# One transformer decoder layer with routed experts: GpSimd handles group 1's rows and routing ahead of group 0's scatters

## The reference

```
x = layernorm(x + attn_block(x))          # linear attention (16 heads of 8) and a GELU FFN
x = layernorm(x + cross_attn(x, ctx))     # softmax attention, per-head norm, rotary queries
x = layernorm(x + ffn(x))                 # 8 experts, two for each token
```

```
h   = mod(int(x[:, 0] + x[:, 1]), 8)                 # first expert of a token
sel = [h, mod(h + 1, 8)]
out = sum over e in sel of 0.5 * (relu(x @ W1[e] + b1[e]) @ W2[e] + b2[e])
```

## Time and profile before

| | us |
|---|---|
| median of 3 runs | 330.95 |
| lowest, highest | 326.02, 331.38 |
| the profiled execution | 324.2 |
| its span, first to last instruction | 322.4 |

### The profile page before, as it was taken

The page is one execution under the profiler, slowest core; times in us unless marked ns, Lnnn a source line. Parts: engine busy times, 40 slices in busy tenths (PEclk is TensorE's granted clock), DMA queues, the critical chain, the costliest instruction groups (busy, mean ns, idle before and its releaser), DMA issues. The chain is left out here.

```text
span 322.4 us, 7292 instructions
## 1 busy us (share of the span) xinstructions
PE 262.2 (81%) x2341; PEld 193.9 (60%) x2341; DVE 179.2 (56%) x634; ACT 152.8 (47%) x375; POOL 117.6 (36%) x191
## 2 busy tenths in 40 slices
PE   0697867878999978788888989595399999999980
PEld 0376656744354346444454555384389999999970
DVE  4641564942025464697778791359336666566650
ACT  2234215345689781557667766312044444444440
POOL 4000004800432441346312717577324333444441
PEclk9999999969999995999999999879599999999996
DMA  7910103810599675327690001051222200000000
GB/s 217 271 43 15 55 0 100 180 17 1 143 237 234 204 142 139 47 63 137 204 198 3 3 3 37 2 157 41 58 53 75 75 25 16 16 19 11 5 16 16
DMA packets 26641, 26.43 MB, mean 82 GB/s; under 512 B 2895, under 2 KB 23120, under 8 KB 26610
## 3 DMA queue, kind: packets, MB, share of 16 engines
q1 hardware_dynamic: 24996, 23.25, 30.1%
q0 software_dynamic: 1328, 2.75, 2.5%
q10 hardware_dynamic: 288, 0.07, 0.1%
HBM read 16.93 MB, written 9.29 MB: 81 GB/s over the span
## 5 line engine op out<-in xcount | busy, mean ns | idle before, releaser
L1200 DVE TENSOR_REDUCE M<-ps 128x4 f32<-128x512 f32 x64 | 42.7, 685 | 16.7 <-PE ps L650 16.6
L1015 ACT ACTIVATE CTX<-ps 128x512 f32<-128x512 f32 x64 | 37.8, 602 | 25.7 <-PE ps L685 18.8
L1056 ACT ACTIVATE KPK<-ps,EB 128x128 f32<-128x128 f32 x80 | 24.7, 359 | 37.1 <-PE ps L827 29.5
L838 PE MATMUL ps<-EW,KPK 128*128 128x128 f32 x320 | 39.5, 276 | 0.0
L827 PE MATMUL ps<-QPK,EW 128*128 x320 | 39.1, 275 | 0.4 <-ACT QPK L1041 0.4
L1528 POOL DMA_INDIRECT out_dram<-ADD,tok_u x21 | 21.1, 1005 | 48.9 <-DVE ADD L1360 48.9
L827 PEld LDWEIGHTS ps<-QPK,EW 128*128 128x128 f32 x320 | 37.3, 192 | 0.7 <-issue 0.7
L838 PEld LDWEIGHTS ps<-EW,KPK 128*128 128x128 f32 x320 | 37.2, 191 | 0.0
L416 PE MATMUL ps<-C 128*128 128x128 f32 x160 | 25.5, 318 | 8.0 <-DMA sorted_scratch<-KVS,posu 8.0
L685 PE MATMUL ps<-QPK,KPK 49*128 49x128 bf16 x256 | 25.3, 219 | 4.8 <-ACT CTX L1015 2.5
L416 PEld LDWEIGHTS ps<-C 128*128 128x128 f32 x160 | 23.4, 228 | 9.4 <-issue 9.0
(11 more groups left out here) (215 smaller groups left out, 495.3 us busy)
## 6 DMA issues: line engine op xcount, KB each, us to landing
k_packed_scratch<-PART SPq DMA_DIRECT2D x24, 128.0 KB, 2.4
KPK<-k_packed_scratch SPq DMA_DIRECT2D x8, 384.0 KB, 6.4
q_packed_scratch<-PART SPq DMA_DIRECT2D x24, 128.0 KB, 2.5
QPK<-q_packed_scratch SPq DMA_DIRECT2D x8, 384.0 KB, 5.8
EW<-in_eW_dram SPq DMA_DIRECT2D x1, 2048.0 KB, 11.4
KPK<-sorted_scratch SPq DMA_DIRECT2D x24, 66.0 KB, 1.8
X<-in_x_dram SPq DMA_DIRECT2D x4, 256.0 KB, 3.9
C<-in_constants_dram SPq DMA_DIRECT2D x1, 720.0 KB, 6.5
```

Source lines behind the costliest of these rows:

```text
L838: last = mm(ps[:, 4, 0:P], HE[:, c, :], EW2[:, e, c % NF, :], start=(c == 0), stop=(c == 2 * NF - 1))
L1015: A(EXPS[:, u % 4, :], ps[:, 2 + u % 2, :], ACT.Exp).then_inc(s_exp, 1)
L1056: last = A(HE[:, c, :], ps[:, k, (c % 2) * P:(c % 2 + 1) * P], ACT.Relu, bias=EB1[:, h, c:c + 1])
L1200: nc.vector.tensor_reduce(M[:, b % RING, c:c + 4], bank_rows(u % 2), AX.X, ALU.max).then_inc(s_max, 1)
```

## The change

On GpSimd the call of `scatter(0)` moves from behind `route(0)` to behind `route(1)`. Nothing else differs: the operations, tiles and semaphores are the same, and the waits within `scatter(0)` stay with it.

```diff
             normalise_rows(0)
             route(0)
-            scatter(0)
             normalise_rows(1)
             route(1)
+            scatter(0)
             scatter(1)
             normalise_rows(2)
             scatter(2)
```

## The result

The changed kernel takes 328.56 us in the median of 20 runs (323.08 to 335.23), the kernel before 327.47 in the median of as many (320.03 to 331.38). The ratio is 1.010, with a 95% interval of 1.006 to 1.014. So it is slower by 1%, where 0.992 was forecast: it moved the other way. That 328.56 us is nearly the forecast 328.4 is luck: the forecast was counted from the 330.95 us of three runs, and twenty runs put the kernel before at 327.47.

The account below looks back on a forecast made before the run. The chain to the sixteenth scatter was taken as bound, with GpSimd's queue limiting after the change: 5.4 us earlier, 3.2 given back, 0.3 added, 2.55 gained. Span 319.9 (318.9 to 320.5; all cases 316.1 to 324.0), median 328.4 us (322.5 to 331.0).

Parts of the forecast that it names:

- step 2: TensorE's and VectorE's chain to posu of group 2 moves 3.61 to 6.3 us earlier, ready between 213.0 and 215.7.
- Step 1: GpSimd starts group 1 at 192.43; route(1) ends at 202.32, 5.4 us earlier, removing TensorE's 3.61 us wait.
- Steps 3 and 4: GpSimd after route(1): gap 0.8, eight scatters 9.93, normalise_rows(2) 3.15, gap 0.8 us, then scatter(2) at 217.05.
- step 4: At scatter(2), GpSimd becomes the bound, starting it 2.55 us earlier; wrong if VectorE still releases it.
- Step 5: The last scatter lands at 228.4 instead of 230.97; register loads and slot loop move earlier as a block.
- rival (b): Slot loop or scatter landing gives part back through TensorE's half clock; net gain 0.6 to 1.3 us; chance 0.17.
- (a): All of the TensorE and VectorE chain's gain reaches the end, 3.6 to 6.3 us; chance 0.08.
- (d): At ranks(1), something other than GpSimd sets TensorE's arrival, so nothing is gained, span 322.4 us; chance 0.05.
- Rival (c): The scatter row between route(1) and normalise_rows(2) grows 4.2 us with its gaps, making the kernel 1.6 us slower; chance 0.08.
- the rule that speaks against the row: VectorE's four float32 TENSOR_SCALAR could lock GpSimd's descriptor port and stretch scatters beside them; rows showed 0.96 us either way.

Follow-up runs that it names:

- after_f: The changed kernel again, no edit, as control in a set with increments on time; ratio 0.993 to the kernel before, 34.7 us from group 1's rstd to the last scatter.
- late set: Runs on one chip whose profiles show TensorE's increments late beside scatters; the changed kernel's ratios to the kernel before there were 1.010, 1.015 and 1.003.
- after: The first profiled execution of the changed kernel, no further edit; span 330.2 us, ratio of its runs to the kernel before 1.010.
- before: The first profiled execution of the kernel before, without the change, from which the forecast was made; span 322.4 us, time 324.2 us.
- set 1: One chip's runs: changed kernel, kernel before, and the changed kernel with scatter(0) held until TensorE's last product with V; changed kernel 0.990 of before, increments on time.
- early_place: Kernel before with place(0) two units earlier, scatter(0) in a row, VectorE writing X2 of group 2; 0.985 of before, increments on time.
- early_place2: The same kernel as early_place, run again in a late set; 1.010 (0.993 to 1.026) of the kernel before.
- fill_dve: Kernel before plus 14 dummy TensorE products in its wait for route(1) and VectorE writing X2 of group 2; 0.987 of before, increments on time.
- before_b: The kernel before again, no edit, in set 1; 36.8 us from group 1's rstd to the last scatter's end.
- before_c: The kernel before again, no edit, in a late set; 37.2 us from group 1's rstd to the last scatter's end.
- row_before2: Kernel before without the waits that space scatter(0), so its four scatters stand in a row, in a late set; 1.012 (1.006 to 1.019) of before.
- 2 and 4: Two sets, each on its own chip, with unedited reruns of the changed kernel beside other variants; changed kernel 1.015 and 1.003 of before.
- row_before: The same kernel as row_before2, run in a set with increments on time; 1.011 (1.001 to 1.020) of the kernel before.

## Why the prediction was wrong

The step that failed is step 2, and with it the overlap that it takes as free.

- **Step 1 was right.** `route(1)` ends 9.98 us after the `rstd` of group 1 in after_f (196.73 to 206.71); the forecast had 202.32 − 192.33 = 9.99. TensorE's wait for it is gone in all profiles of the changed kernel.
- **Step 2 failed, in a late set.** It says that TensorE's and VectorE's chain moves "by at least the 3.61 us of the wait". It took for granted that TensorE's products beside the scatters finish as they did beside GpSimd's small operations. From L735 of group 1 to `posu` of group 2 after shows 209.32 to 227.27 = 18.0 us, against 11.4 in before; in after_f it is 208.18 to 217.43 = 9.25, near the 8.8 that the step has at full clock (11.44 less 2.67). The missing term is the 3.3 to 6.2 us of late increments and the half clock behind them; the step put it at nothing.
- **Steps 3 and 4 were right where increments are on time.** Gap after `route(1)` 0.74 (0.8 taken), row 10.0 (9.93), `normalise_rows(2)` 3.1 to 3.3 (3.15), gap before scatter(2) 0.78 in after_f (0.8). That GpSimd releases `scatter(2)` holds in the sets on time alone; in the late ones it is VectorE, the sign that the prediction gave for step 4 being wrong. The net of the stretch in set 1, on time, is 36.8 less 34.8 or 34.7, 2.0 to 2.1 us, where 2.55 was forecast from before, whose stretch is 37.2; the intervals of the ratios 0.990 and 0.993 hold 0.992.
- **Step 5 and rival (b).** From the last scatter's end to the end of the span it is 92.9, 93.9 and 94.2 us in the three profiles of the kernel before, and 92.7 to 93.8 in the seven of the changed kernel. TensorE's longer idle time (11.5 us in after_f) cost nothing that can be seen. Rival (b) falls. So do (a), since in after_f GpSimd's L1463 and not VectorE releases `scatter(2)`, and (d), since the wait at L735 is gone.
- **Rival (c) had the right place and the wrong victim.** It asked whether the row would be slow. The row keeps 0.30 us between scatters everywhere; what slows is TensorE beside it. The same mistake stands in the paragraph on the rule that speaks against the row: I looked at the scatters' own durations beside VectorE, found them even, and took the overlap as free for all engines. Even for the scatters it is not quite even: where VectorE's four `TENSOR_SCALAR` of group 2 still run as a row starts (early_place, early_place2, fill_dve), its first scatter took 1.20 to 1.21 us, against 1.10 without.

The trace of before had a sign of it. Beside its first two scatters (192.00 and 193.41 us), timelines of TensorE and VectorE, not among the rows shown ahead:

```profile
193.64 0.44 PE L723 MATMUL ps<-C,V 128*128 128x128 f32 x2
...
198.31 0.41 PE L723 MATMUL ps<-C,V 128*128 128x128 f32 x2 [0.51 <-ACT QP L993]
```

```profile
194.87 0.26 DVE L1205 RECIPROCAL RD<-ps 128x16 f32<-128x16 f32 x1 [1.51 <-PE ps L723]
...
198.76 0.26 DVE L1205 RECIPROCAL RD<-ps 128x16 f32<-128x16 f32 x1 [3.30 <-PE ps L723]
```

VectorE follows the second L723 0.04 us after its end and the first 0.79 us after. In before_b, of a set on time, it follows the same L723 beside the same scatters after 0.03 us:

```profile
201.54 0.44 PE L723 MATMUL ps<-C,V 128*128 128x128 f32 x2
```

```profile
202.01 0.26 DVE L1205 RECIPROCAL RD<-ps 128x16 f32<-128x16 f32 x1 [0.74 <-PE ps L723]
```

before_c, of a late set, has 0.79 us there as well. So before was itself an execution of the late kind. Its `scatter(0)` comes spaced by TensorE's own units, the lateness met slack, and the price didn't show. The waits for units 50 to 56 that I called "long satisfied" kept `scatter(0)` from standing in a row.

## What to carry to other kernels

When work moves on one queue, look at what the other engines do beside its new place, and compare the time from an instruction's end to the start of its waiter, there and elsewhere: a lateness that slack hides now is the price once slack is gone. Indirect DMAs in a row beside TensorE's small dependent products can cost more than their own time (3.3 to 6.2 us beside a row of 10 here), and where TensorE's clock falls behind the delay, that can be the larger part (row_before2). And measure a change of 1% in several sets: here its sign depended on the set.

## What the runs showed of the hardware

- In three of six sets, counting the result's as one (the result's, 2 and 4), TensorE's semaphore increments arrive late while GpSimd issues indirect DMAs at a spacing of 1.26 us: by up to 0.8 us with two in a row (before; the expectations above say 1.1), 2.9 and 3.6 with four (row_before2, early_place2), 3.3 to 6.2 with eight (the changed kernel). In the other three sets they are never late with the same kernels.
- What is late seems to be the increment and not the product: in after VectorE, which waits for an L723 issued behind the last L707, starts 0.04 us after ScalarE, less than the 0.44 us that these transposes take. This is inferred from two rows, not shown by an experiment.
- Sixteen scatters land with 256 increments of `s_sort`. The traces of late sets hold fewer records of them: 91, 92, 110 and 84 in those of the changed kernel, against 250 to 253 in those on time; 131 and 137 against 256 for the kernel before. So the recording of events may have a part in it, and whether the lateness is there in an execution that isn't recorded stays open, as does what makes one set late and another not. That four of the five ratios follow the kind speaks for it, and the ratios of row_before and row_before2 do not.
- After such a delay the granted clock fell to 0.50: for 10.2 us in after, starting within an idle time of TensorE of 4.47 us; for 17.1 us in row_before2, behind idle times of 0.63 and 1.33 us; for 23.9 us in early_place2, behind 1.33, 0.33 and 0.44. The Trainium skill (TensorE: Matmul & The Clock Gate, Part 1) states that idle time throttles TensorE's clock; the falls agree with it in kind. In early_place2 the clock stayed at 0.50 from 210 to 220 us although the profile has TensorE busy for all 10.00 us. Falls of 17 to 31 us stand in the attention units too, ahead of any scatter and in both kinds of set (before_b 145.1 to 175.8, after 142.8 to 173.6), so how much of a fall's length comes from the delay ahead of it is not shown.
